# Attention layers with routed experts: a batch's two row scatters sent at two places of GpSimd's period

## The reference

```python
x = x + xattn_0(layernorm(x), ctx, ...)   # 16 heads of 8, masked softmax(q k^T) v, output product
x = x + ffn_0(layernorm(x), ...)          # 8 experts, the 2 best of each row, silu
x = x + xattn_1(layernorm(x), ctx, ...)   # rope on q and k, a window of 64 keys
x = x + ffn_1(layernorm(x), ...)          # 8 experts, the 2 best of each row, and a shared expert
```

## Time and profile before

| | before |
|---|---|
| time, median of 3 runs | 693.52 us (693.27 to 696.43) |
| span of the profiled execution | 763.9 us, the one time that the profile gives for it |
| busy: PE, DVE, ACT, POOL | 671.5, 523.5, 415.8, 504.9 us (88%, 69%, 54%, 66% of the span) |
| mean granted TensorE clock | 0.953 |
| scatters (L626) | 128 DMAs, 991 ns each on POOL, 126.9 us in all |
| chain that ended last | PE 50%, POOL 17%, issue 12%, DVE 8%, ACT 5% |

### The profile page before, as it was taken

How to read it: one execution, slowest core, us unless ns; L and a number is a source line. 1 busy time by engine, 2 the same in 40 slices (tenths; PEclk the granted TensorE clock), 3 DMA queues, 4 the chain that set the end, 5 groups by cost and what they waited for, 6 DMA issues and landing times.

```text
span 763.9 us, 21054 instructions
## 1 busy us (share of the span) xinstructions
PE 671.5 (88%) x7092; PEld 546.5 (72%) x7092; DVE 523.5 (69%) x1515; ACT 415.8 (54%) x1158; POOL 504.9 (66%) x837
## 2 busy tenths in 40 slices
PE   8799998888876999999979999888888668788797
PEld 7567666665646999999957776666667568778787
DVE  5489988888663446555358898888886555555556
ACT  5477767654542434444447777656547445555563
POOL 5975788577564678877677778777667635455451
PEclk9899999999997999999979999999989989899999
DMA  5470000001331522343110101111211312222264
GB/s 166 124 305 2 17 27 27 27 30 36 137 99 48 160 70 81 97 127 89 46 36 29 30 26 40 54 37 37 66 34 37 89 51 77 61 75 72 75 232 152
DMA packets 45406, 57.78 MB, mean 76 GB/s; under 512 B 11379, under 2 KB 37142, under 8 KB 44630
## 3 DMA queue, kind: packets, MB, share of 16 engines
q1 hardware_dynamic: 36086, 38.17, 16.6%
q0 software_dynamic: 8640, 17.97, 7.1%
q10 hardware_dynamic: 576, 0.29, 0.1%
HBM read 33.82 MB, written 22.08 MB: 73 GB/s over the span
## 4 chain that ended last, share of the span: by engine, by line
PE 50%; POOL 17%; issue 12%; DVE 8%; ACT 5%; another core or an unknown queue 4%; DMA 2%; SPq 1%; DVEq 0%; POOLq 0%; ACTq 0%
POOL results L1625 9%; PE ptp L1349 8%; PE M L1366 7%; PE ptp L2078 6%; PE S L1326 5%; PE S L2059 5%; PE S L1330 3%; PE ptp L1352 3%; POOL xi L1618 2%; POOL rows L626 2%; PE M L1374 2%; PE M L1418 2%; PE S L2065 1%; SPq L707 1%
## 5 line engine op out<-in xcount | busy, mean ns | idle before, releaser
L626 POOL DMA_INDIRECT rows<-out_rows,posi x128 | 126.9, 991 | 50.1 <-issue 32.1
L806 ACT ACTIVATE pT<-ptp 128x512 f32<-128x512 f32 (+1 forms) x192 | 95.1, 525 | 97.7 <-PE ptp L1349 87.0
L1929 POOL DMA_INDIRECT results<-early,xs x71 | 69.0, 971 | 68.4 <-DVE early L2001 50.9
L1064 DVE TENSOR_REDUCE mx<-S 128x16 f32<-128x1232 f32 x64 | 91.3, 1427 | 18.3 <-PE S L1330 16.4
L1625 POOL DMA_INDIRECT results<-early,xi x71 | 75.9, 1069 | 40.5 <-DVE early L1687 35.1
L1065 DVE TENSOR_TENSOR pr<-S,mx 128x1232 f32<-128x1232 f32 x64 | 92.3, 1442 | 2.2
L1724 PE MATMUL S<-first_w,early 128*128 x568 | 77.2, 279 | 3.0 <-DVE early L1687 1.5
L1714 PE MATMUL S<-early,w1s 128*128 128x128 f32 x568 | 76.9, 279 | 0.6 <-ACT early L1659 0.6
L1366 PE MATMUL M<-pT,vm 128*32 128x128 f32 (+1 forms) x2048 | 74.7, 283 | 1.1 <-ACT pT L806 0.6
L1349 PE MATMUL ptp<-cst,pr 128*128 128x128 f32 x512 | 74.0, 290 | 0.0
L1724 PEld LDWEIGHTS S<-first_w,early 128*128 128x128 f32 x568 | 69.5, 193 | 5.9 <-issue 5.7
(11 more groups left out here) (221 smaller groups left out, 1527.9 us busy)
## 6 DMA issues: line engine op xcount, KB each, us to landing
xs<-rows SPq DMA_DIRECT2D x142, 66.0 KB
first_w<-in_e_W SPq DMA_DIRECT2D x2, 2048.0 KB, 8.2
swap<-results SPq DMA_DIRECT2D x32, 128.0 KB
first_w<-results SPq DMA_DIRECT2D x6, 512.0 KB
rows<-out_rows,posi POOLq DMA_INDIRECT x128
x_res<-in_x SPq DMA_DIRECT2D x1, 1536.0 KB, 8.4
W1r<-in_e_W SPq DMA_DIRECT2D x1, 1536.0 KB, 10.8
out_x<-x_res SPq DMA_DIRECT2D x3, 512.0 KB, 2.7
```

The source lines that it names most:

```text
L626: nc.gpsimd.indirect_dma_start(rows[:, :], bass.IndirectOffsetOnAxis(posi[:, k, n:n + 1], 0), out_rows[:, ring_slot(groups, n), k, :], Non ...
L806: nc.scalar.activation(pT[0:rows_of, G * r:G * r + count, :], ptp[q % 2][0:rows_of, 0:count, :], ACT.Exp, scale=SCALE)\
L1064: do(V.tensor_reduce(mx[:, :].rearrange("p (g j) -> p g j", g=G), sc, AX.X, ALU.max))
```

## The change

A period's scatters are sent at two places. At the end of period k, as before, goes copy 0 of the batches that are due (with the index, where a group begins). Copy 1 of the same batches goes in period k + 1: behind that period's take_results or norms, turn_queries and keys, and ahead of its padded_values, and only when TensorE has signalled the scores of batch k + 2 in the semaphore's count, that is of the batch with index k + 1. This holds for periods up to 30 (`apart`): 20 periods with 24 batches in layer 0, 18 periods with 20 batches in layer 1. In later periods both copies go together as before.

```diff
@@ -615,14 +615,18 @@
                                     zero[:, 0:1].unsqueeze(1).unsqueeze(1).broadcast_to([128, size, 2, 1]), ALU.add)\
                 .then_inc(idx_set, 1)
 
-        def scatter(n):
+        def apart(k):
+
+            return k < B - 1 and len(sends.get(k, ())) > 0
+
+        def scatter(n, copies=(0, 1)):
 
             g = group_of(groups, n)
-            if n == groups[g][0]:
+            if n == groups[g][0] and 0 in copies:
                 index(g)
                 pool.wait_ge(pos_ready, g + 1)
                 pool.wait_ge(idx_set, g + 1)
-            for k in range(2):
+            for k in copies:
                 nc.gpsimd.indirect_dma_start(rows[:, :], bass.IndirectOffsetOnAxis(posi[:, k, n:n + 1], 0),
                                              out_rows[:, ring_slot(groups, n), k, :], None).then_inc(scattered[lane(groups, g)], 16)
 
@@ -655,6 +659,10 @@
                 turn_queries(k + 1)
             for n in range(keys_made(k - 1), keys_made(k)):
                 keys(n)
+            if apart(k - 1):
+                wait(pool, s_ready, min(k + 2, B))
+                for n in sends[k - 1]:
+                    scatter(n, (1,))
             for n in (0, 1) if k == 0 and not rope else (k + 1,):
                 if k >= 0 and live(n):
                     padded_values(n)
@@ -667,7 +675,7 @@
             if sends.get(k) and 1 <= k <= B:
                 pool.wait_ge(pv_done, k)
             for n in sends.get(k, ()):
-                scatter(n)
+                scatter(n, (0,) if apart(k) else (0, 1))
             yield k
 
     def k_copy(act, c):
```

## The result

The changed kernel takes 718.41 us (median of 4 runs, 718.04 to 722.85) against 694.49 us (4 runs, 693.27 to 696.43): ratio 1.0349, 95% interval 1.0325 to 1.0372, some 24 us slower. The forecast was 705.5 us, with a range up to 721 and a rival, no lateness in a run, at 717.5. The sign was right and the size half of what came.

A forecast was written before the change was run, and what follows sets the result against it. Copies that make TensorE's signals late were taken to cost 40 us, all the change could win. Terms -4, +7 and +3 gave +6 us on the profiled execution, +12 in a run: 705.5 us, range 692 to 721.

The forecast's parts named there:

- no lateness in a run: Rival, whole kernel: late signals come only from the profiler, old layer 1 step 5.35 us; +24 us, 717.5 us, chance 0.20.
- the ring: Layer 1, GpSimd: queries, scores, second copy, padded_values, first copy, norms or results wait in turn; 6.6 us a step.
- A: Layer 0, periods 11 to 30: moved copies trade 0.76 us of lateness a step for some 0.5; -4 us.
- B: Layer 1, periods 14 to 30: the second copy's wait makes steps 6.6 us where they were 6.16; +7 us.
- C: End of layer 1: two more copies behind a wait for the last scores delay the last norms; +3 us.
- The old step: Layer 1 with scatters, before the change: taken as 6.16 us from the first profile.
- From the profiled execution to a run: Whole kernel: a third of the lateness taken as the profiler's, turning +6 us into +12.
- late signals: Both layers: TensorE's signals taken to come 0.6 to 0.9 us late by where a copy falls; 40 us winnable.
- +2 if norms are late: Layer 0, an end of its estimate: norms behind the shifted first copy delay the normalisation in a few steps; +2 us.
- the first copy's new place: Layer 0: the first copy would fall over the value products and make their signal late; 0.62 us.
- Copies do not delay TensorE: Rival: something else made exponentials late, layer 0 gains 0; +10 us, 703.5 us, chance 0.10 shared with layer 0 unchanged.

The follow-up runs named there:

- no_wait: The changed kernel with the second copy at its new place but without its wait for the scores, both layers; ratio 1.0017 to the kernel before.
- l1_behind: The changed kernel with the split in layer 1 alone, wait and second copy moved behind padded_values and the first copy; ratio 0.9990 to the kernel before.
- the second profile: The kernel before, unchanged, profiled once more; 694.93 us, span 693.1 us.
- l0_to_22: The changed kernel with the split in layer 0 alone and only up to period 22; ratio 1.0064 to the kernel before.
- l1_only: The changed kernel with the split in layer 1 alone; ratio 1.0246 to the kernel before, +17 us.
- l1_to_26: The changed kernel with the split in layer 1 alone and only up to period 26; ratio 1.0271 to the kernel before.

## Why the prediction was right on the ring and wrong on the size

**The ring in layer 1** was forecast as it came. The order of instructions and the durations in the rows gave it, and its length of 6.6 to 6.7 us is 6.66 in the period shown and 6.53 on average. That the wait and not the copy's place makes it is shown from three sides: without the wait (no_wait) and with the wait behind the other work (l1_behind) the loss is gone, and some 0.5 us more on the ring adds 0.54 us a step where the clock is the same.

**The sum.** In the terms of the prediction, between the two profiled executions: A came out at +3.4 where -4 stood, B at +14.4 where +7 stood, C at +4.8 where +3 stood. That is 22.6 instead of 6. The last step of the working added 6 for the profiler, which makes the forecast's +12 against +23.1.

**The old step** is where the sum failed, in "From the profiled execution to a run". It took a third of the late signals for the profiler's, and so two thirds of them as real in a run; the second profile has none of them. (Its steps with copies do cost 18 us more than as many quiet ones, not 40, but not through late signals.) The old step in layer 1 is 5.74 us and not 6.16, so the same ring costs 9.5 us in its middle instead of 5, and its last steps 4.9 instead of 2, some 1.4 of that at a lower clock. The sign that this execution was no measure stood in the first paragraph: its span was some 10% above every run. The working spread the 70 us "over the whole span"; but eight quiet steps take 39.10 us in the second profile and took 39.09 in the first, so what was extra sat in particular places, the steps with copies among them. The largest place was another: 41.4 of the 70.8 us between the two executions lie behind layer 1's last products, in the tail and the experts (189.8 against 148.4 us, at a granted clock of 0.92 against 0.98). The bounds then had to be worked from the quiet steps and GpSimd's own list, which is what the rival at 717.5 did.

**Term A** was wrong in both its halves. There was no lateness to win, and the cost that was named only as an end ("+2 if norms are late") became the whole: +0.8 in the first twelve steps, +2.6 in the next eight. That nothing of GpSimd's list stands between one batch's scores and the next's holds for the queries. But the norms are on that list, ScalarE's normalisation waits for them and its exponentials stand behind the normalisation; and the list is full where two batches are due, so a delay that reaches these periods is paid there. Nor is the first copy's new place the costly one: in the changed kernel the value products are copied 0.06 to 0.16 us after their end in all 64 batches, never 0.69. The sign given for layer 0, steps of 5.2 to 5.5 us, came true by luck: they are 5.35 and 5.52, but up from 5.28 and 5.19 and not down from 5.65 and 6.34. In layer 0's tail the working said no copy is added ahead of the last norms, hence 0; these norms came 1.7 us later against the last products by the same backlog. What that costs is not sure, as the +1.7 of the stretch behind is not clear of its spread, and l0_to_22, whose last norms are only 0.5 us later, is as long there (253.2).

**Term C** had the right mechanism and was too small. From the last queries to the last norms are 567.33 - 553.48 = 13.85 us where the kernel before has 544.78 - 535.42 = 9.36: +4.5, and +4.8 behind the last products, for a forecast of +3. The saved 1.00 us of the earlier trace rows isn't there in the second profile. The timelines, changed kernel first:

```profile
553.48 0.45 POOL L605 TENSOR_TENSOR qT<-swap 128x128 f32<-128x128 f32 x1
...
567.33 0.21 POOL L552 TENSOR_TENSOR negm<-mv,cst 128x4 f32<-128x4 f32 x1
```

```profile
535.42 0.45 POOL L605 TENSOR_TENSOR qT<-swap 128x128 f32<-128x128 f32 x1
...
544.78 0.21 POOL L552 TENSOR_TENSOR negm<-mv,cst 128x4 f32<-128x4 f32 x1
```

**The rivals.** "No lateness in a run" was right to 1 us in its total, with errors that cancel: 21 us for the ring where 14.4 came (its old step of 5.35 is GpSimd's list alone, and VectorE holds the step at 5.74), and 0 for layer 0 where 3.4 to 5 came. "Copies do not delay TensorE" was right in what it says: in the second profile the starts behind TensorE keep their quiet distance with copies and without. Its price, +10, was not, for it kept the old step at 6.16. The rule that "SBUF — State Buffer" of the Trainium skill gives in "Who interferes with whom", that TensorE and ScalarE wait for nobody, agrees with these exponentials 0.69 us behind the transposes, with one copy ahead of the transposes and one over them; the rows that seemed to speak against it came from one disturbed execution. What disturbed it stays open. The Trainium skill, "Perfetto Trace Analysis", section "Tensor Engine Instruction (MATMUL, LD_WEIGHTS)", adds a caution: TensorE's reported end is estimated from the instruction's size and an SBUF delay, and not observed. So a late start behind a usual 1.09 us did not show, as the prediction said, that the signal was late and not the work.

## What to carry to other kernels

A wait that is put into an engine's list closes a ring when the waited-for work needs something that the same list makes further down; its length is the sum of all that lies on it, and it can be worked out beforehand, from the order and the durations. Put such a wait behind the work on the list that does not need the signal: in layer 1 the same wait costs 17 us ahead of padded_values and the first copy, and nothing that can be told behind them. And set the span of a profile beside the times of the runs first: if it is 10% above all of them, take another profile before any price is read from it.

## What the runs showed of the hardware that was not expected

TensorE's clock fell in one execution and not in another, at the same place and behind the same idle time. The same batch's step, at 496.85 in the changed kernel and at 492.99 in l1_only, has TensorE idle for 2.1 us before its scores in both, waiting for qT, as the timelines show, the changed kernel first:

```profile
500.27 0.80 PE L1334 MATMUL S<-first_w,qT 32*128 32x308 f32 x8 [2.14 <-POOL qT L605]
```

```profile
496.40 1.41 PE L1334 MATMUL S<-first_w,qT 32*128 32x308 f32 x8 [2.13 <-POOL qT L605]
```

In the one the granted clock stayed at 1.00 (2.4 GHz) and the step took 7.42 us; in the other it fell within the idle time and was 0.50 (1.2 GHz) from the scores on until the value products, 0.66 on the step's average, the first transposes taking 1.97 us in place of 1.09, and the step took 10.13. The windows of all engines for that step (us, then busy time of PE, PEld, DVE, ACT and POOL, then the clock), changed kernel first:

```profile
496.85:504.27 7.42, 5.28 (x74) 3.81 (x74) 6.83 (x15) 3.28 (x8) 5.35 (x10) 1.00 0.06 20
```

```profile
492.99:503.12 10.13, 8.00 (x74) 5.81 (x75) 8.56 (x29) 3.39 (x8) 7.07 (x12) 0.66 0.06 22
```

So such an idle time cost 2.7 us more than its length at one time and not at another. Totals of kernels with the ring can differ by a few us for it: l1_to_26, whose layer 1 is l1_only's up to period 26, takes 7.38 us for this step where l1_only takes 10.13, and 8.68 at a granted clock of 0.80 for another where l1_only takes 7.34 at 1.00. What made the clock fall in one and not in the other stays open.
